# Constant products behind each tile's scores in the four self attentions of a four-layer Perceiver

## The chip, the cores and the metric

One NeuronCore of a Trainium2 chip runs the whole program in one launch. The metric is the device time of that launch in microseconds, and where several runs stand, their median. TensorE is called PE below (its weight loads PEld), VectorE DVE, ScalarE ACT, GpSimd POOL and the queue that issues transfers SP.

## What is computed

The program is a chain of twelve residual blocks on `x` of 32 sequences x 32 tokens x 256 channels, in four layers of cross attention, self attention (or a convolution with pooled keys) and a feed-forward or mixture of experts. The change touches the self attentions only. There are four: in layer 0 (`L0_attn`, causal, scores from three pairs of features), layer 1 (`L1_attn`, relu in place of softmax), layer 3 (`L3_attn`, causal) and, inside the last block, `L3_gqa` (softmax). Cut to the core, each is

```
q, k, v = x @ Wq, x @ Wk, x @ Wv          # 16 heads of 16 channels
a = einsum('bqhd,bkhd->bhqk', q, k) / 4   # 32 x 32 for each sequence and head
a = softmax(where(causal, a, -inf))       # L1_attn: relu(a) / (sum(relu(a)) + 1e-6)
x = x + einsum('bhqk,bkhd->bqhd', a, v) @ Wo
```

## The kernel before

All 1024 tokens lie on chip as 8 tiles (`NT`) of 128 tokens, four sequences to a tile (`BT`). Every block of the network is one or more stages. A stage is a set of five instruction streams, one for each engine, that start together and meet again at its end; within it an engine runs its stream in the order in which it is written, and waits on semaphores where `wait_ge` stands. `prepare` normalises, transposes and projects; `self_attention` follows it.

`self_attention` works through the tiles i = 0 to 7. The order is written out by hand. On PE a tile has five parts:

- `scores(i)` (L1487): small products of 32 rows x 64 columns that sit side by side in the array, 32 of them in float32 (96 in `L0_attn`, with its three feature sets); the causal ones start with 8 products that write the mask (L1479). Their queries are written as block patterns by `spread_queries` on ACT (L1554), DVE (L1616) and POOL (L1599).
- `turn_probs(i)` (L1496): four transposes of the probabilities, which DVE (L1622, L1624) and ACT (L1563, for relu L1560) make from the scores. ACT then copies them out of PSUM (L1570).
- `probs_values(i)` (L1505): 64 products of 32x32 by 17 columns.
- `turn_outputs(i)` (L1512): two transposes of the outputs that DVE normalised (L1634, L1636), copied by ACT.
- `output_product(i)` (L1521): two full products, 128x128 by 256 columns.

The float32 products show in the trace as two matmuls each, the transposes as one. The stream is skewed: with the probabilities of tile i turned, PE does the scores of tile i+1, so that DVE and ACT can make the next probabilities meanwhile; then the outputs of tile i-1 are turned, the values of tile i are multiplied, and the output product of i-1 is made. PSUM bank 6 (`OB`) holds the turned outputs in its first 256 columns; the other 256 are unused. `k.ident` and `k.consts` are constants that stay on chip during the whole program.

All of this is written out for all tiles, without a loop, so that PE's instruction stream is long, and it is itself brought in by transfers from memory (queue q8 of the profile, 16 KB each).

Of the kernel before, what the change touches and what calls it, by code (L numbers as in the profile page):

```python
# [24 lines left out]
B, S, D = 32, 32, 256  # L25
# [267 lines left out]
def spread(ap, n, axis):  # L293

    shape = list(ap.shape)
    return ap.unsqueeze(axis).broadcast_to(shape[:axis] + [n] + shape[axis:])
# [1150 lines left out]
def self_attention(k, w, qt, kt, v, into, causal=False, relu=False, scale=0.25, more=(), after=None):  # L1447

    nc = k.nc
    sets = [(qt, kt), *more]  # L1450
    SB, TB, PB, OB, YB = 0, 4, 5, 6, 7
# [4 lines left out]
    with stage(k, names) as (block, s), \  # L1456
# [13 lines left out]
        @block.tensor  # L1470
        def _(pe):
            def scores(i):
                for done in spread_by:
                    pe.wait_ge(done, i + 1)
                if causal:
                    for r in range(4):
                        rows = slice(r * S, (r + 1) * S)
                        for c in range(DC):
                            nc.tensor.matmul(k.ps[c * 64:(c + 1) * 64, SB + r, 0:P], k.same[rows, :],  # L1479
                                             spread(k.causal[rows, :], BT, 1), start=True, stop=False, skip_group_check=True)  # L1480
                for b_ in range(BT):
                    for m, (_, keys) in enumerate(sets):
                        for r in range(4):
                            rows = slice(r * S, (r + 1) * S)
                            for c in range(DC):
                                own = i * P + b_ * S
                                last = nc.tensor.matmul(k.ps[c * 64:(c + 1) * 64, SB + r, b_ * S:(b_ + 1) * S],  # L1487
                                                        b.qx[rows, i % 2, m, c, b_, :, :], keys[rows, c, own:own + S],
                                                        start=m == 0 and not causal, stop=m == len(sets) - 1,
                                                        skip_group_check=True)  # L1490
                last.then_inc(s.scores_done, 1)

            def turn_probs(i):
                pe.wait_ge(s.probs_ready, i + 1)
                for r in range(4):
                    last = nc.tensor.transpose(k.ps[:, TB, r * P:(r + 1) * P], b.p[:, r, :, :].rearrange("p b l -> p (b l)"),  # L1496
                                               k.ident)
                last.then_inc(s.turned_done, 1)

            def probs_values(i):  # L1500
                pe.wait_ge(s.turned_ready, i + 1)
                for h in range(16):
                    for b_ in range(BT):
                        rows = slice(b_ * S, (b_ + 1) * S)
                        last = nc.tensor.matmul(k.ps[rows, PB, h * 17:(h + 1) * 17], b.pt[rows, h % 8 // 2, h // 8, h % 2, :],  # L1505
                                                v[rows, i, h, :], start=True, stop=True)
                last.then_inc(s.pv_done, 1)

            def turn_outputs(i):
                pe.wait_ge(s.o_ready, i + 1)  # L1510
                for c in range(DC):
                    last = nc.tensor.transpose(k.ps[:, OB, c * P:(c + 1) * P],  # L1512
                                               b.o[:, c * 8:(c + 1) * 8, :].rearrange("p h d -> p (h d)"), k.ident)
                last.then_inc(s.ot_done, 1)

            def output_product(i):
                pe.wait_ge(s.ot_ready, i + 1)
                if i > 0:
                    pe.wait_ge(s.y_added, i)
                for c in range(DC):  # L1520
                    last = nc.tensor.matmul(k.ps[:, YB, 0:D], b.ot[:, c, :], w.wo[:, c, :], start=c == 0, stop=c == DC - 1)  # L1521
                last.then_inc(s.y_done, 1)

            pe.wait_ge(*w.at)
            scores(0)
            pe.wait_ge(s.ones_set, 1)
            for i in range(NT):
                turn_probs(i)
                if i + 1 < NT:
                    scores(i + 1)  # L1530
                if i > 0:
                    turn_outputs(i - 1)
                probs_values(i)
                if i > 0:
                    output_product(i - 1)
            turn_outputs(NT - 1)
            output_product(NT - 1)
            if after == "turned":
                for half in range(2):
                    for t in range(4):  # L1540
                        pe.wait_ge(s.z_ready, half * 4 + t + 1)
                        for c in range(DC):
                            last = nc.tensor.transpose(k.ps[:, 2 * half + c, t * P:(t + 1) * P],
                                                       into[:, half * 4 + t, c * P:(c + 1) * P], k.ident)
                    last.then_inc(s.z_turned, 1)
# [1480 lines left out]
```

## Time and profile before

| | us |
|---|---|
| three runs | 1976.07, 1983.77, 1986.21 |
| median | 1983.77 |
| the profiled execution, its span | 1979.5 |
| `L0_attn`, self attention stage | 300.7 to 400.8 |
| `L1_attn` | 864.5 to 920.1 |
| `L3_attn` | 1683.5 to 1742.4 |
| `L3_gqa` | 1766.8 to 1824.4 |

The times of the stages are from the span's start, in the profiled execution. A "busy" PE counts matmul records; PEclk is the clock that was granted to it, as a share of its full 2.4 GHz, so that 0.50 is 1.2 GHz. "issue" as the reason of a wait means that PE waited for nothing that the profile shows.

### The profile page before, as it was taken

The page shows a single profiled execution, that of the slowest core. Times are in us where ns is not written, and L with a number is a line of the kernel's source. Part 1 is how long each engine was busy: PE and PEld are TensorE (multiplying, and loading weights), DVE is VectorE, ACT ScalarE, POOL GpSimd, SP SyncE. Part 2 cuts the span into 40 slices and gives each one's busy share as a digit, 9 for nine tenths or more (in the row PEclk, how much of TensorE's full clock was granted, in tenths as well). Part 3 has the DMA queues.
Part 4 walks back from the last instruction along what each step waited for, and adds up shares of the span by engine and source line. Part 5 has one row for each costly group of instructions (what it writes and reads, how often), then busy time and mean ns, then how long its engine had stood idle before and what let it go on. Part 6 is the DMA issues. An engine that isn't in the chain of part 4 may idle for free. (4 is left out here: it accounts for less than half of the span.)

```text
span 1979.5 us, 53753 instructions
## 1 busy us (share of the span) xinstructions
PE 1634.6 (83%) x22089; PEld 1401.9 (71%) x22089; DVE 956.7 (48%) x2107; ACT 748.1 (38%) x1700; POOL 447.5 (23%) x627
## 2 busy tenths in 40 slices
PE   6999846769997899887699949997698988778695
PEld 5888645659995777675588848994686966666584
DVE  5565373241115888535512156664666744434313
ACT  3555372123342555432133326663124423333122
POOL 3443102012222434110244322220101200010242
PEclk8999855569998999876699979998898979776697
DMA  4111000049982211001599753331001163000596
GB/s 140 51 52 30 5 1 3 4 177 325 326 316 100 56 51 46 8 6 47 175 311 312 264 182 94 93 89 46 4 19 40 42 199 128 4 2 4 169 306 220
DMA packets 82023, 219.99 MB, mean 111 GB/s; under 512 B 19160, under 2 KB 35032, under 8 KB 74656
## 3 DMA queue, kind: packets, MB, share of 16 engines
q1 hardware_dynamic: 69888, 191.11, 29.6%
q0 software_dynamic: 8160, 22.29, 3.0%
q10 hardware_dynamic: 3776, 3.67, 0.6%
q8 instruction: 158, 2.59, 0.5%
q14 instruction: 41, 0.34, 0.1%
HBM read 201.62 MB, written 15.34 MB: 110 GB/s over the span
## 5 line engine op out<-in xcount | busy, mean ns | idle before, releaser
L2308 PEld LDWEIGHTS ps<-xt,w 128*128 128x128 f32 x1728 | 208.0, 196 | 36.1 <-issue 29.8
L2308 PE MATMUL ps<-xt,w 128*128 128x128 f32 x1728 | 215.9, 282 | 18.7 <-DMA w<-in_L_ffn_w 15.8
L2360 ACT ACTIVATE g<-ps,b 128x128 f32<-128x128 f32 x340 | 124.8, 367 | 247.7 <-PE ps L2308 226.3
L2318 PE MATMUL ps<-w,g 128*128 128x256 f32 x864 | 201.9, 381 | 0.6 <-DMA w<-in_L_ffn_w 0.6
L2318 PEld LDWEIGHTS ps<-w,g 128*128 128x128 f32 x864 | 158.8, 192 | 19.0 <-DMA w<-in_L_ffn_w 1.1
L2396 POOL DMA_INDIRECT x<-rows,token x85 | 83.1, 978 | 261.6 <-DVEq L2496 236.7
L2401 POOL DMA_INDIRECT results<-y,dest x85 | 83.6, 984 | 258.3 <-DVE y L2529 258.3
L2521 DVE COPY xt<-ps 128x256 f32<-128x256 f32 x85 | 36.1, 425 | 202.7 <-PE ps L2298 202.7
L2529 DVE COPY y<-ps 128x256 f32<-128x256 f32 x85 | 36.1, 425 | 162.6 <-PE ps L2318 162.6
L761 PE MATMUL ps<-c,w 128*128 128x258 f32 x512 | 97.2, 302 | 9.9 <-DVE pt L1068 5.9
L761 PEld LDWEIGHTS ps<-c,w 128*128 128x128 f32 x512 | 77.6, 196 | 23.7 <-issue 19.4
L771 PE MATMUL ps<-w,c 128*128 128x256 f32 x512 | 91.2, 291 | 0.0
L897 ACT ACTIVATE p<-sc,nmax 128x257 f32<-128x257 f32 x128 | 58.0, 503 | 80.6 <-DVE nmax L1025 80.6
L407 PE MATMUL ps<-consts_sb,z_sb 128*128 128x128 f32 x176 | 38.8, 411 | 58.4 <-DVE z_sb L591 58.4
L1013 DVE TENSOR_TENSOR val<-ps,store_sb 128x512 f32<-128x512 f32 x64 | 44.2, 690 | 84.7 <-PE ps L771 84.5
L425 PE MATMUL ps<-x,w 128*128 128x512 f32 x336 | 80.7, 399 | 4.5 <-DVE x L603 4.5
L2006 PE MATMUL ps<-x,w 128*128 128x512 f32 x288 | 77.0, 407 | 7.7 <-DVE w L2169 7.7
L570 POOL TENSOR_TENSOR w<-store_sb,w 128x512 fp32r<-128x512 f32 (+1 forms) x20 | 27.0, 1365 | 240.9 <-DVE z_sb L591 205.3
L407 PEld LDWEIGHTS ps<-consts_sb,z_sb 128*128 128x128 f32 x176 | 34.7, 219 | 63.7 <-DVE z_sb L591 63.1
L797 PE MATMUL ps<-consts_sb,p 128*128 128x128 f32 x512 | 74.7, 281 | 5.1 <-ACT key L887 2.2
L2019 PEld LDWEIGHTS ps<-w,g 128*128 128x128 f32 x576 | 74.8, 191 | 5.4 <-issue 1.5
L425 PEld LDWEIGHTS ps<-x,w 128*128 128x128 f32 x336 | 63.7, 192 | 19.6 <-DVE x L603 6.7
(447 smaller groups left out, 3660.7 us busy)
## 6 DMA issues: line engine op xcount, KB each, us to landing
w<-in_L_ffn_w SPq DMA_DIRECT2D x124, 512.0 KB, 5.0
w<-in_L_ffn_w SPq DMA_DIRECT2D x46, 1024.0 KB, 6.0
c<-in_ctx SPq DMA_DIRECT2D x96, 258.0 KB, 2.7
rows<-in_w_L_xattn SPq DMA_DIRECT2D x32, 192.0 KB, 2.6
rows<-in_w_L_xattn SPq DMA_DIRECT2D x8, 768.0 KB
c<-in_w_L_xattn SPq DMA_DIRECT2D x8, 514.0 KB
raw<-in_L_ffn_w SPq DMA_DIRECT2D x16, 256.0 KB, 2.8
tails<-in_w_L_xattn SPq DMA_DIRECT2D x5, 768.0 KB, 7.3
```

Of the source, the lines that this page charges most:

```text
L407: mm = nc.tensor.transpose(k.ps[:, 2 * half + c, t * P:(t + 1) * P], z[:, half * HT + t, c * P:(c + 1) * P], k.ident)
L425: mm = nc.tensor.matmul(bank, r.w[:, p1, c, col:col + P], r.x[:, p2, c, half * 512:(half + 1) * 512], start=i == 0 and c == 0, stop=i == 2 ...
L761: last = nc.tensor.matmul(k.ps[:, KB + c, 0:LP], wp, cp, start=t == 0, stop=t == 4)
L771: last = nc.tensor.matmul(k.ps[:, VB, half * D:(half + 1) * D], cp, wp, start=t == 0, stop=t == 4)
L797: last = nc.tensor.transpose(k.ps[:, TB + pair, at:at + P], b.p[:, par, r4, half * P:(half + 1) * P], k.ident)
L2006: mm = nc.tensor.matmul(k.ps[:, slot(j, h), :], r.w1[:, j // 2, p1, c, h * P:(h + 1) * P], r.x[:, p2, c, (j % 2) * 512:(j % 2 + 1) * 512], ...
L2019: mm = nc.tensor.matmul(k.ps[:, 4 + t, 0:D], r.g[:, p1, slot(j, h), t * P:(t + 1) * P], r.w2[:, j // 2, p2, h, :], start=h == 0 and i == 0 ...
L2308: mm = nc.tensor.matmul(hidden_bank(par, h), b.w1[:, par, c, h * P:(h + 1) * P], b.xt[:, par, c, :], start=c == 0, stop=c == DC - 1)
L2318: mm = nc.tensor.matmul(k.ps[:, YB + par, 0:D], b.g[:, par, h, :], b.w2[:, par, h, :], start=h == 0, stop=h == HC - 1)
L2360: nc.scalar.activation(b.g[:, par, h, :], hidden_bank(par, h), func, bias=b.b1[:, par, h:h + 1]).then_inc(s.g_ready, 1)
L2396: nc.gpsimd.indirect_dma_start(b.x[:, n % 4, :], None, k.rows, bass.IndirectOffsetOnAxis(ap=u.token[:, n:n + 1], axis=0)).then_inc(x_loade ...
L2401: nc.gpsimd.indirect_dma_start(k.results, bass.IndirectOffsetOnAxis(ap=u.dest[:, n:n + 1], axis=0), b.y[:, n % 2, :], None).then_inc(sent[ ...
```

## The change

A helper `keep_awake(n)` issues n float32 products on PE: the identity as the stationary operand, the first 256 columns of the constants as the moving one, into the unused half of PSUM bank 6. Nothing waits for them and nothing reads them. They stand in three places: two at a stage's start, ahead of the wait for the weights; five behind the first tile's scores (two for relu); and two behind the scores of each later tile. That makes 21 products in three of the stages and 18 in `L1_attn`, 81 in all.

```diff
@@ -1521,13 +1521,21 @@
                     last = nc.tensor.matmul(k.ps[:, YB, 0:D], b.ot[:, c, :], w.wo[:, c, :], start=c == 0, stop=c == DC - 1)
                 last.then_inc(s.y_done, 1)
 
+            def keep_awake(n):
+
+                for _ in range(n):
+                    nc.tensor.matmul(k.ps[:, OB, D:2 * D], k.ident, k.consts[:, 0:D], start=True, stop=True)
+
+            keep_awake(2)
             pe.wait_ge(*w.at)
             scores(0)
+            keep_awake(2 if relu else 5)
             pe.wait_ge(s.ones_set, 1)
             for i in range(NT):
                 turn_probs(i)
                 if i + 1 < NT:
                     scores(i + 1)
+                    keep_awake(2)
                 if i > 0:
                     turn_outputs(i - 1)
                 probs_values(i)
```

On PE, at the start of `L0_attn` and behind its first scores (`ps<-consts_sb` of 64x128 is the causal mask, the last row turns the first probabilities):

```order
 L1470 UNCONDITIONAL_BRANCH
+L1527 MATMUL ps<-consts_sb 128x256 x2
 L1479 MATMUL ps<-consts_sb 64x128 x8
 L1487 MATMUL ps<-qk,qx 64x32 x8
...
 L1487 MATMUL ps<-sn,qx 64x32 x8
 L1487 MATMUL ps<-cs,qx 64x32 x8
+L1527 MATMUL ps<-consts_sb 128x256 x5
 L1496 MATMUL ps<-consts_sb,p 128x128 x4
```

Two products now stand ahead of the first scores and five between the first scores and the transposes that wait for the first probabilities.

On PE, one tile inside `L1_attn` before:

```order
L1496 MATMUL ps<-consts_sb,p 128x128 x4
L1487 MATMUL ps<-kt,qx 64x32 x32
L1512 MATMUL ps<-consts_sb,o 128x128 x2
L1505 MATMUL ps<-v,pt 32x17 x64
L1521 MATMUL ps<-store_sb,ot 128x256 x2
```

and the same tile now:

```order
L1496 MATMUL ps<-consts_sb,p 128x128 x4
L1487 MATMUL ps<-kt,qx 64x32 x32
L1527 MATMUL ps<-consts_sb 128x256 x2
L1512 MATMUL ps<-consts_sb,o 128x128 x2
L1505 MATMUL ps<-v,pt 32x17 x64
L1521 MATMUL ps<-store_sb,ot 128x256 x2
```

The two products come between the scores of the next tile and the turned outputs of the last one; nothing else on PE changes its place, and the other engines' streams are the same.

## Rows read from the trace of the kernel before

**Rows 1.** The page: span, and the clock granted to PE in 40 slices.

```profile
span 1979.5 us, 53753 instructions
...
PEclk8999855569998999876699979998898979776697
```

**Rows 2.** Stretches, the four stages: length, busy time (count) of PE, PEld, DVE, ACT, POOL, PEclk, DMA.

```profile
300.70:400.80 100.10, 72.59 (x2768) 60.50 (x2768) 28.08 (x70) 21.85 (x43) 15.06 (x17) 0.55 0.01 4
...
864.50:920.10 55.60, 49.85 (x1619) 40.07 (x1617) 19.30 (x53) 18.31 (x41) 5.67 (x2) 0.57 0.02 4
...
1683.50:1742.40 58.90, 46.89 (x1744) 38.16 (x1744) 23.11 (x54) 21.85 (x43) 0.32 (x1) 0.70 0.02 4
...
1766.80:1824.40 57.60, 46.48 (x1616) 37.68 (x1616) 21.88 (x53) 21.57 (x42) 4.69 (x2) 0.61 0.02 4
```

**Rows 3.** Stretches of one tile, L1496 to L1496, and sums of seven: L0_attn.

```profile
332.50:344.46 11.96, 8.69 (x348) 0.64 0.02 4
344.46:356.12 11.66, 9.18 (x347) 0.50 0.01 3
...
sum 81.28, PE 60.98; mean PE 8.71
```

**Rows 4.** The same of L1_attn, all engines.

```profile
887.86:894.28 6.42, 6.42 (x204) 5.19 (x203) 2.28 (x7) 2.25 (x5) 0.00 (x0) 0.50 0.01 3
...
sum 45.32, PE 43.43 PEld 35.31 DVE 12.10 ACT 14.66 POOL 3.75; mean PE 6.20 PEld 5.04 DVE 1.73 ACT 2.09 POOL 0.54
```

**Rows 5.** The same of L3_attn.

```profile
1693.93:1700.89 6.96, 6.96 (x225) 5.74 (x219) 2.75 (x6) 2.38 (x5) 0.00 (x0) 0.50 0.02 5
...
1720.32:1725.55 5.23, 4.33 (x219) 3.68 (x218) 3.01 (x7) 2.38 (x5) 0.00 (x0) 1.00 0.03 6
...
sum 45.71, PE 37.83 PEld 31.36 DVE 18.64 ACT 15.52 POOL 0.00; mean PE 5.40 PEld 4.48 DVE 2.66 ACT 2.22 POOL 0.00
```

**Rows 6.** The same of L3_gqa.

```profile
sum 44.18, PE 40.51 PEld 32.96 DVE 17.94 ACT 15.52 POOL 0.00; mean PE 5.79 PEld 4.71 DVE 2.56 ACT 2.22 POOL 0.00
```

**Rows 7.** Timeline of PE, L1_attn: start, length, line, shape, count [idle before].

```profile
885.99 2.07 PE L1521 MATMUL ps<-store_sb,ot 128*128 128x256 f32 x4
887.86 1.06 PE L1496 MATMUL ps<-consts_sb,p 128*128 128x128 f32 x4
```

**Rows 8.** Timeline of PE, L3_attn (clock 1.00 until past 1728.60).

```profile
1723.74 0.91 PE L1505 MATMUL ps<-v,pt 32*32 32x17 f32 x87 [0.90 <-issue]
1724.58 1.13 PE L1521 MATMUL ps<-store_sb,ot 128*128 128x256 f32 x4
1725.55 0.60 PE L1496 MATMUL ps<-consts_sb,p 128*128 128x128 f32 x4
1726.08 0.47 PE L1479 MATMUL ps<-consts_sb 32*64 32x128 f32 x16
1726.35 0.29 PE L1487 MATMUL ps<-kt,qx 32*64 32x32 f32 x16
1727.58 0.72 PE L1487 MATMUL ps<-kt,qx 32*64 32x32 f32 x48 [0.94 <-issue]
1728.23 0.44 PE L1512 MATMUL ps<-consts_sb,o 128*128 128x128 f32 x2
1728.60 0.84 PE L1505 MATMUL ps<-v,pt 32*32 32x17 f32 x78
1731.05 0.88 PE L1505 MATMUL ps<-v,pt 32*32 32x17 f32 x50 [1.61 <-issue]
```

**Rows 9.** Waits of PE in L0_attn: us in total, times, longest.

```profile
PE ps L1487 <- issue: 11.5, 8, 2.1
PE ps L1479 <- POOL qx L1599: 8.7, 1, 8.7
PE ps L1505 <- issue: 8.0, 7, 1.3
PE ps L1496 <- ACT p L1563: 2.3, 1, 2.3
```

**Rows 10.** Waits of PE in L3_gqa.

```profile
PE ps L1496 <- ACT p L1563: 5.4, 1, 5.4
```

## The prediction

> **What bounds the kernel now.** I first read the span and the row of the granted clock [rows 1]: PE is at full clock for most of the program, and slices 7 and 8, in which `L0_attn` lies, are among the lowest, with 5 tenths. Next I cut out the four stages that the change touches [rows 2]. They take 100.1, 55.6, 58.9 and 57.6 us, 272.2 us of 1979.5, and PE's clock in them is 0.55, 0.57, 0.70 and 0.61. PE is the busiest engine in each; DVE, ACT and POOL are busy for less than half. So PE's stream sets their length, and the rest of the program isn't touched.
>
> Within PE there are two limits, and the reader has to see both. The first is the clock. In `L1_attn` a tile takes 6.42 us with PE busy for 6.42 of them, at 0.50 [rows 4]: nothing waits, the engine is just slow. The same groups are quicker at full clock: from the start of the output product to the start of the next transposes it is 1.87 us at 1.2 GHz [rows 7] and 0.97 us at 2.4 GHz [rows 8].
>
> The second limit shows as soon as the clock is full. At 1.00, a tile of `L3_attn` has 4.33 us of work but takes 5.23 [rows 5], and the timeline has waits for "issue" of 0.90, 0.94 and 1.61 us [rows 8]. They aren't scattered: from the end of one to the start of the next there are 87+4+4+16+16 = 127 matmuls, then 48+2+78 = 128, and the ends are 3.84 and 3.47 us apart. Such a regular count speaks for the stream being brought in by pieces of 128 matmuls with their weight loads, each 3.65 us behind the last at best. In `L0_attn` these waits are 11.5 + 8.0 us of the 100 [rows 9], and a tile at clock 0.64 isn't shorter (11.96) than one at 0.50 (11.66) [rows 3]. There a faster array only waits longer.
>
> **The added products at one tile.** Two float32 products of 128x128 by 256 columns are what the output product is. I take them at the same 1.87 us for a pair at 1.2 GHz and 0.97 at 2.4 GHz [rows 7, 8]. PE is the engine that everything waits for, so by themselves they are paid in full where PE has no waits, as in `L1_attn`, and hidden where a wait for instructions stands behind them, since the next piece comes in meanwhile. They add 4 matmuls to a piece's count, which is small. DVE isn't held: the semaphore of the scores is raised by the last score, ahead of the added products.
>
> **What they do to the clock.** The change takes nothing away, so a gain can only come from here. In the trace, the clock rises after stretches in which full-array work lies close together, and falls after stretches of scores and values, small products that leave most of the array idle even where PE is busy the whole time: in `L1_attn` the seven tiles had PE busy for 43.43 of 45.32 us [rows 4] and nearly all at 0.50. A tile now has one such stretch, the output product and the next transposes, 8 matmuls. With the pair behind the scores it has a second, half a tile away. I expect that this lifts the clock early in a stage and then mostly holds it, as it already held for one whole tile of `L3_attn` (1.00) with half the work [rows 5]. I take 9 tiles of 10 at full clock in `L1_attn`, `L3_attn` and `L3_gqa`; the bounds are all and none.
>
> The Trainium skill, "TensorE: Matmul & The Clock Gate" ("Why this matters for your kernels"), speaks against this change: it ties the full clock to keeping TensorE busy without gaps. By that rule a PE that is busy already, as in `L1_attn`, gains nothing from more work. The tile at 6.42 us busy of 6.42 and at 0.50 doesn't agree with the rule as a matter of busy time alone; where it held, the sum would be the rival of the cold clock below.
>
> **The sum.** At full clock, a tile is the longer of its work and its pieces. Work: 4.33 us in `L3_attn` [rows 5] + 0.97 = 5.3; less in the others, which have no mask. Pieces: `L1_attn` and `L3_gqa` have 202 matmuls in a tile and now 206, so 206/128 x 3.65 = 5.9 us; `L3_attn` has 222, so 6.3 us. The pieces win. At half clock, a tile is 6.42 + 1.87 = 8.3 us, and 6.96 + 1.87 = 8.8 us in `L3_attn` [rows 4, 5].
>
> - `L1_attn`: 45.32/7 = 6.47 us a tile now [rows 4]. Full: 7 x (5.9 - 6.47) = -4.0; half: 7 x 1.83 = +12.8. With 9 to 1: -2.3 us.
> - `L3_gqa`: 44.18/7 = 6.31 [rows 6]. Full: -2.9; half: +13.9. With 9 to 1: -1.2 us.
> - `L3_attn`: 45.71/7 = 6.53 [rows 5], it was at 0.70 already. Full: -1.6; half: +16. With 9 to 1: +0.2 us.
> - `L0_attn`: 81.28/7 = 11.61 [rows 3]. Waits for pieces in front of the values are 8.0/7 = 1.14 us a tile [rows 9]; they stand right behind the new pair. At half clock 1.87 - 1.14 = 0.73 shows, at full clock 0.97 is hidden. This stage has few output products for its length, and I leave it mostly at half clock: +0.5 a tile, +3.5 us. Bounds: +13 (nothing hidden, 7 x 1.87) and -3 (the clock rises and some of it isn't eaten by the pieces).
> - The starts. The first pair is hidden: PE waits 8.7 us for POOL's queries in `L0_attn` [rows 9]. The five behind the first scores take 2.5 x 1.87 = 4.7 us at half clock. In `L3_gqa` they lie in a wait of 5.4 us [rows 10], hidden. In `L0_attn` the wait for the first probabilities is 2.3 us [rows 9] and the clock is low: +2.4. In `L3_attn` the clock is full and they take 2.4 us, which about fills the same wait; `L1_attn`, with two, pays some 0.2.
>
> Sum: -2.3 - 1.2 + 0.2 + 3.5 + 2.4 + 0.2 = +2.8 us on the execution of 1979.5, which lies 4.3 below the median of the runs. On the median of 1983.8 it gives 1986.6; I say 1986.
>
> **The rivals.** *The clock stays low* (slower). The pair doesn't lift it, or only as often as now. Then each of the three short stages pays its half-clock figure, 12.8 + 13.9 + 16, of which `L3_attn` and `L3_gqa` hide a part in their present waits for pieces (some 7 in all), and `L0_attn` 7 x 0.73 + 2.4 = 7.5: about +43, 2027 us. For it: the tile in `L1_attn` that is busy throughout at 0.50. Against: the clock does rise in these stages, after the output products, and the pair is of that shape. Half of it (the clock up for 6 tiles of 10) would give some +20, 2004; the point from which it shows as slower is about 7 tiles of 10 at full clock.
>
> *The pieces aren't a floor* (faster). If the waits for instructions shrink because the added products give the transfers time, tiles come near their work at full clock: 5.3 us in `L3_attn` and some 4.9 in the two others, which is 7 x (1.2 + 1.6 + 1.4) = -29, and with `L0_attn` at -3 some -30: 1954. Half of it is 1969. For it: 4.33 us of work in the tile at 1.00. Against: the two ends 3.84 and 3.47 us apart, which a product in between doesn't shorten.
>
> *The change does not reach the time*: the products are nearly all hidden and the clock as now; that is within 5 us of the median too and is counted with "same".
>
> **How the numbers follow.** A measurement of this kernel can tell about 0.5%, 10 us, from no change. My forecast and its near neighbours, 1974 to 1994: 0.58. The faster rival in whole or in part: 0.20. The clock too low, in whole or in part: 0.22. Range: from 1966 (half of the faster one) to 2006 (half of the slower one), which leaves out about 0.1 at each side.
>
> **What would show it.** In the profile after: the added line with 162 matmuls; the clock in the four stages (I expect 0.9 or more in the three short ones, and 0.6 to 0.75 in `L0_attn`); tiles of 5.8 to 6.3 us with waits for "issue" left, some 128 matmuls apart. Tiles over 8 us with PE busy throughout at 0.50 would show the slower rival, tiles under 5.5 us the faster one. The forecast is wrong in its first step if another stage than these four moves by more than the few us that separate the runs.

## The result and the profile after

The changed kernel takes 1970.08 us (median of 20 runs, 1961.32 to 1981.43), the one before 1978.79 us (20 runs, 1969.25 to 1986.73). The ratio is 0.9962 with a 95% interval of 0.9947 to 0.9977: 7.5 us faster, by 4.6 to 10.5. The forecast was 1986 and a small loss. The time lies inside the range, but the sign was wrong, and by more than the interval.

The page after, span and granted clock, against [rows 1]:

```profile
span 1966.9 us, 54077 instructions
...
PEclk9999956779998999888799969998898989988697
```

The four stages, cut as in [rows 2] (length, busy time and count of PE, PEld, DVE, ACT, POOL, then PEclk and DMA):

```profile
300.10:394.10 94.00, 73.94 (x2810) 61.31 (x2810) 28.04 (x71) 20.98 (x42) 15.06 (x17) 0.72 0.02 4
850.40:907.50 57.10, 48.44 (x1655) 38.72 (x1654) 19.24 (x53) 18.33 (x41) 5.69 (x2) 0.85 0.02 4
1671.20:1726.70 55.50, 46.78 (x1786) 38.34 (x1786) 23.82 (x55) 20.97 (x42) 0.32 (x1) 0.97 0.02 4
1750.90:1810.10 59.20, 49.98 (x1658) 40.39 (x1658) 22.56 (x55) 20.97 (x42) 4.71 (x2) 0.83 0.02 4
```

The clock rose in all four, from 0.55, 0.57, 0.70 and 0.61 to 0.72, 0.85, 0.97 and 0.83. But the stage that I had given a loss of 6 us, `L0_attn`, is 6 us shorter, and `L1_attn`, with a much higher clock, is no shorter at all. (The last two stretches begin with the first added products, 1 us ahead of where they began before. From ACT's first query pattern to the last output product the four stages take 93.4, 55.7, 54.4 and 58.2 us, against 99.4, 54.2, 58.8 and 57.5.)

The added line in the list of groups, and what PE waited for in `L0_attn`, against [rows 9] (us in total, times, longest):

```profile
L1527 PE MATMUL ps<-consts_sb 128*128 128x256 f32 x162 | 55.4, 479 | 8.3 <-PEq L223 8.3
```

```profile
PE ps L1487 <- issue: 13.2, 7, 2.3
PE ps L1527 <- PEq L223: 5.1, 1, 5.1
PE ps L1479 <- issue: 3.2, 6, 0.7
PE ps L1505 <- issue: 1.6, 2, 0.9
```

55.4 us of matmuls were added to a program that became shorter. The waits for instructions in front of and inside the values (L1505) fell from 8.0 to 1.6 us: the pair lies where they were. Those at the scores didn't fall (11.5 and 1.5 us before, for L1487 and for L1479; 13.2 and 3.2 now).

Two traces don't settle a few us. Stages that the change does not touch differ as well between them: the products of `L1_xattn`'s cross attention, from the first to the last on PE, took 207.2 us in the trace before, 6.9 us less in the one after, and 1.4 to 6.0 us less in those of the five experiments of the whole program below, none of which touches it. So the experiments measure the whole program many times, or the same stage several times in one trace.

### The profile page after: what moved, and what is told of

Same layout as the page of the kernel before. It is cut to its first block and busy times, and to the rows that moved or that the text cites. A ratio compares the mean times of both kernels' runs of the same rounds, so it can differ in the third digit from the quotient of the medians.

```text
span 1966.9 us, 54077 instructions
## 1 busy us (share of the span) xinstructions
PE 1633.8 (83%) x22251; PEld 1397.4 (71%) x22251; DVE 956.8 (49%) x2107; ACT 746.9 (38%) x1700; POOL 447.0 (23%) x627
## 5 line engine op out<-in xcount | busy, mean ns | idle before, releaser
L897 ACT ACTIVATE p<-sc,nmax 128x257 f32<-128x257 f32 x128 | 58.0, 503 | 80.5 <-DVE nmax L1025 80.5
L407 PE MATMUL ps<-consts_sb,z_sb 128*128 128x128 f32 x176 | 39.3, 415 | 58.8 <-DVE z_sb L591 58.8
```

What stands on the lines that cost most here:

```text
L407: mm = nc.tensor.transpose(k.ps[:, 2 * half + c, t * P:(t + 1) * P], z[:, half * HT + t, c * P:(c + 1) * P], k.ident)
```

## The experiments

Ratios are to the kernel before, run on the same chip; the experiments were spread over two chips. "A stage" is from ACT's first query pattern to the last output product.

### In which stage is the gain?

Two kernels share the added products out. The first keeps them in `L0_attn` only, the second everywhere else.

```diff
-                for _ in range(n):
+                for _ in range(n if len(sets) > 1 else 0):      # e1_first_only
+                for _ in range(n if len(sets) == 1 else 0):     # e2_not_first
```

> The added products stand in L0_attn alone (21 of the 81). Theory 1 (the step of my sum that failed is L0_attn: its clock rises from 0.55 to about 0.7, and the rise is not eaten by the waits for instructions): L0_attn, 99.5 us from its first query pattern to its last output product, comes down to 93 to 95, and the program is at a ratio of 0.996 to 0.998. Theory 2 (L0_attn gains nothing, as predicted, and the gain is made in the short stages or between the stages): L0_attn at 99 or more, ratio 1.000 to 1.003.

> The added products stand in L1_attn, L3_attn and L3_gqa and not in L0_attn. Theory 1: the three stages together are within 3 us of before, the ratio is 0.998 to 1.001. Theory 2: the ratio is near 0.996, as with the whole change.

`L0_attn` alone: 1975.02 us, ratio 0.9973 (0.9952 to 0.9993). The other three alone: 1976.08 us, ratio 0.9985 (0.9961 to 1.0009). The two add up to what the whole change gives (0.27% + 0.15% and 0.38%). So there is a gain in the one stage to which I had given the largest loss, and the first theory stands in its direction. That it is the larger part of the whole isn't shown: the two intervals overlap, and the second one holds no change as well. The size in this one trace, 97.9 us against 99.4, was smaller than expected; the four-fold runs below give 2.9 us.

### The starts

The pair behind the scores of tiles 1 to 7 is dropped, and the products at the stage's start and behind its first scores are kept.

```diff
                     scores(i + 1)
-                    keep_awake(2)
```

> Only the products at the start of each stage and behind its first scores (25 of the 81), none in the later tiles. If the clock is held by the pair of each tile: after the first tiles the clock is as before, the stages gain at most 1 to 2 us each, ratio 0.998 to 1.001. Rival, that lifting the clock once at the start is what counts: ratio near 0.996.

1982.75 us, ratio 1.0008 (0.9986 to 1.0031). Lifting the clock once gives nothing that can be measured. The gain needs the pairs; whether they would do without the products at the starts no run shows.

### The array's work or only the time?

The same number of products of the same length, but in one corner of the array:

```diff
-                    nc.tensor.matmul(k.ps[:, OB, D:2 * D], k.ident, k.consts[:, 0:D], start=True, stop=True)
+                    nc.tensor.matmul(k.ps[0:32, OB, D:2 * D], k.ident[0:32, 0:32], k.consts[0:32, 0:D], start=True, stop=True)
```

> The whole change, but each added product uses 32 rows and 32 columns of the array, by the same 256 columns of data: the same number of matmuls and the same length of each (an estimate from the wide ones: 1.9 us a pair at 1.2 GHz), with a sixteenth of the array at work. Theory of the clock: it stays as low as before or lower (0.5 to 0.6 in the four stages), every tile is 1 to 2 us longer, and the program is 25 to 45 us slower (ratio 1.013 to 1.023). Rival, that the products help by giving the instruction transfers time, whatever they compute: ratio 0.996, like the change.

1989.27 us, ratio 1.0058 (1.0037 to 1.0080): slower by 11 us, and about 1% slower than the wide products. The sign is the clock theory's; the size is less than half of what I expected of it, and it isn't the rival's 0.996 either. The clock that I had expected, 0.5 to 0.6 in all four stages, was so in `L0_attn` alone: the trace has 0.58, 0.78, 0.66 and 0.75. How much of that is the one trace shows in the next set.

### Four samples of each stage

To see a stage by itself, each of the four self attention stages is run four times in a row, in the kernel before, in the change, and in two variants. The output is then another one, the stages are not.

```diff
-                    self_attention(k, w, b.qk[:, 0], ...)
+                    for _ in range(4):
+                        self_attention(k, w, b.qk[:, 0], ...)   # and the same for the three others
```

> The kernel before with each of the four self attention stages run four times in a row, so that one trace holds four samples of each stage with the clock in different positions (the output is then not the reference's). It is the baseline for the three next. Stages as before within 3 us: L0_attn 99, L1_attn 50 to 54, L3_attn 55 to 59, L3_gqa 57 to 60, and the program some 3 x 265 = 800 us longer.

> The change, with each self attention stage run four times in a row (output not the reference's). If the gain lies in the stages themselves, it shows four times: 4 x 5 to 9 us = 20 to 36 us less than the same kernel before, half of it in the four passes of L0_attn (3 to 5 us each). If most of it came from the stages behind them or from chance, 0 to 10 us less.

> The same with narrow products (32 rows and 32 columns of the array), each self attention stage four times (output not the reference's). Clock theory: the clock in the stages is below the wide ones' by 0.1 or more and each stage is 4 to 8 us longer than with wide ones. Rival (the products only give the instruction transfers time): the same as the wide ones within 1 us a stage.

> The change with the pair of each tile moved from behind the scores to behind the output product, each self attention stage four times (output not the reference's). If the place in front of the values is what hides the pair (it lies in the wait for instructions there), L0_attn is 3 to 6 us longer than with the pair behind the scores, and has its waits of 1.1 us in front of or inside the values back. If only the full-array work counts, it is the same within 1 us.

The last one has the pair moved:

```diff
                 if i + 1 < NT:
                     scores(i + 1)
-                    keep_awake(2)
...
                 if i > 0:
                     output_product(i - 1)
+                if i + 1 < NT:
+                    keep_awake(2)
```

The medians are 2839.37 us (before), 2816.86 (change), 2909.29 (narrow) and 2872.35 (behind the output product). All four ran on one chip. The change is 22.5 us faster, which is 5.6 for each pass through the four stages; the narrow products are 70 us slower than none, and the pair in the other place 33 us slower. Means of the four passes of a stage, in us, with the clock:

| | before | change | narrow | behind output |
|---|---|---|---|---|
| `L0_attn` | 97.3, 0.58 | 94.4, 0.71 | 103.0, 0.58 | 99.0, 0.71 |
| `L1_attn` | 54.3, 0.67 | 55.4, 0.84 | 58.1, 0.70 | 58.6, 0.79 |
| `L3_attn` | 59.1, 0.67 | 55.1, 0.96 | 64.8, 0.68 | 60.5, 0.87 |
| `L3_gqa` | 56.0, 0.68 | 57.1, 0.87 | 61.5, 0.69 | 59.4, 0.84 |
| sum | 266.7 | 262.0 | 287.4 | 277.5 |

The passes of one stage in one trace lie 2 to 6 us apart (`L0_attn` in the change: 91.9, 94.1, 97.2 and 94.3), so a mean of four is good to 1 us or so, as an estimate. The losses of 1.1 us in `L1_attn` and `L3_gqa` are no larger than that.

The stretch of the four passes of `L0_attn`, with the columns of [rows 2]; before, change, narrow, behind the output product:

```profile
301.20:694.40 393.20, 278.88 (x11072) 233.81 (x11072) 113.82 (x285) 87.00 (x171) 59.81 (x68) 0.58 0.02 4
```

```profile
301.20:682.90 381.70, 302.04 (x11240) 249.41 (x11240) 113.69 (x285) 84.61 (x171) 60.06 (x68) 0.71 0.02 4
```

```profile
300.00:716.40 416.40, 346.31 (x11240) 253.98 (x11240) 113.68 (x285) 84.95 (x172) 60.05 (x68) 0.59 0.01 4
```

```profile
298.80:699.00 400.20, 306.64 (x11240) 254.30 (x11240) 113.86 (x286) 87.14 (x171) 59.80 (x68) 0.71 0.02 4
```

The four passes of `L3_attn` with the narrow products:

```profile
2203.80:2467.20 263.40, 246.12 (x7144) 174.26 (x7144) 95.44 (x221) 84.64 (x171) 1.29 (x4) 0.68 0.01 4
```

And the waits for instructions in `L0_attn`, in the order of its four rows:

```profile
PE ps L1487 <- issue: 49.6, 32, 2.2
PE ps L1505 <- issue: 30.0, 29, 2.3
PE ps L1479 <- issue: 6.3, 24, 0.4
```

```profile
PE ps L1487 <- issue: 48.7, 27, 2.4
PE ps L1479 <- issue: 11.1, 25, 0.7
PE ps L1505 <- issue: 6.0, 8, 1.4
```

```profile
PE ps L1487 <- issue: 48.1, 30, 2.3
PE ps L1479 <- issue: 6.6, 24, 0.5
PE ps L1505 <- issue: 2.5, 3, 1.4
```

```profile
PE ps L1505 <- issue: 41.9, 28, 2.6
PE ps L1487 <- issue: 37.8, 31, 2.3
```

Read across, these rows take the change apart into two mechanisms:

- *Place.* Behind the scores, wide or narrow, the pair takes the wait at the values from 30.0 us to 6.0 or 2.5. Behind the output product, at the same clock of 0.71, the wait is 41.9, and `L0_attn` is 4.6 us a pass longer. Over all four stages the place is worth 15.5 us a pass (277.5 against 262.0), but in the other three the clock is lower as well (0.79, 0.87 and 0.84 against 0.84, 0.96 and 0.87), so only `L0_attn` shows the place by itself.
- *The array's work.* Narrow and wide products stand in the same place and take the same time: in `L0_attn`, from the start of a pair to the next transposes, 1.84 us narrow and 1.87 wide where the clock is at 0.50, 0.98 and 0.97 where it is at 1.00. With the narrow ones the clock stays at 0.58 to 0.70, the values of before, and the four stages take 25.4 us more a pass. PE was busy for 346.31 of 416.40 us in `L0_attn` with the narrow products and only for 302.04 of 381.70 with the wide ones, and the clock was the lower one of the two; in `L3_attn` it was 246.12 of 263.40 us, at 0.68, and 188.26 of 224.70 us with the wide ones, at 0.96. Time occupied isn't what the clock follows. A narrow product has fewer rows, fewer columns and a smaller weight load (123 ns against 190 in the median); which of the three counts isn't shown.

With narrow products each stage was to be 4 to 8 us longer than with wide ones; it was 2.7 to 9.7. In the single kernel they cost 11 us and not 20.7 (287.4 - 266.7), beyond its interval of 7 to 16. The four stages aren't the reason: in the trace of that kernel they take 287.2 us together, as here. What is outside them takes 1701.7 us there and 1709.5 in the trace of the kernel before; in the traces of the change and of the other variants that part, which none of them touches, is between 1705.2 and 1717.0. Why it was short with the narrow products stays open.

### How many products?

One product and four instead of the pair, again in four passes:

```diff
-                    keep_awake(2)
+                    keep_awake(1)      # x4_one;  x4_four: keep_awake(4)
```

> One added product behind each tile's scores, each self attention stage four times (output not the reference's). If the clock needs the pair, it falls back half way (L3_attn 0.8, L0_attn 0.65) and L3_attn is at 56 to 58 us, L0_attn at 94.5 to 96. If one is enough, the clock stays at 0.96 and 0.71, and all four stages are as with the pair or up to 2 us shorter.

> Four added products behind each tile's scores in place of two, each self attention stage four times (output not the reference's). If 128 matmuls of the stream can't come in faster than in some 3.65 us and this bounds L3_attn at full clock (6.3 us a tile, with work of 5.3), the second pair's 0.97 us a tile is mostly hidden: L3_attn 55 to 57.5 us against 55.1 with one pair. If the tile is bound by its work, 7 x 0.97 is added: 61 to 62 us. L0_attn has nearly no wait left in front of its values, so there the second pair shows: 98 to 101 us against 94.4.

One: 2849.70 us; four: 2837.12 us; none was 2839.37 and two 2816.86. But these two kernels ran twice each, on another chip, where the single kernel before takes 1980.22 us and not 1975.49. As ratios to that, none, one, two and four are 1.4368, 1.4387, 1.4273 and 1.4324, each to within 0.006 to 0.008, which doesn't tell one or four products from none. By stage (none, one, two, four): `L0_attn` 97.3, 98.9, 94.4, 97.6; `L1_attn` 54.3, 56.3, 55.4, 55.4; `L3_attn` 59.1, 59.3, 55.1, 54.9; `L3_gqa` 56.0, 56.6, 57.1, 59.0.

The four passes of `L3_attn`, with no product, one, two and four:

```profile
2172.80:2413.50 240.70, 190.63 (x6976) 156.42 (x6976) 95.39 (x222) 87.10 (x171) 1.28 (x4) 0.67 0.02 4
```

```profile
2179.90:2421.50 241.60, 204.99 (x7088) 164.73 (x7088) 95.37 (x221) 86.90 (x172) 1.30 (x4) 0.80 0.02 4
```

```profile
2158.70:2383.40 224.70, 188.26 (x7144) 153.32 (x7144) 95.44 (x221) 84.48 (x171) 1.29 (x4) 0.96 0.02 4
```

```profile
2175.10:2398.80 223.70, 204.95 (x7256) 170.97 (x7256) 95.36 (x222) 84.62 (x171) 1.29 (x4) 0.99 0.02 4
```

The last two rows are the test of the floor in my forecast. The second pair adds 16.7 us of busy PE and the stretch gets 1 us shorter: at full clock a tile of `L3_attn` was not bound by its work. Taken alone, the tiles went from 6.28 to 6.40 us, which is what four more matmuls cost at 128 in 3.65 us (0.11); the stage's start and end made up for it. Its waits for instructions with two and with four products show where the pair went:

```profile
PE ps L1505 <- issue: 21.9, 24, 1.5
PE ps L1487 <- issue: 5.7, 11, 0.9
```

```profile
PE ps L1487 <- issue: 7.1, 13, 1.2
PE ps L1505 <- issue: 3.4, 6, 1.5
```

21.9 became 3.4. The waits themselves bear out the pieces: with two products there are 36 "issue" waits in these four passes, and from each to the next within its pass there are one or two times 128 matmuls (to within one). Where it is 128, 24 times, they are 3.47 to 4.02 us apart, in the median 3.75. One product isn't half of two in `L0_attn`: it leaves the clock at 0.60 and only costs its time. I had expected 0.65 and 94.5 to 96 us there, and 56 to 58 in `L3_attn`, for 98.9 and 59.3; with four products the two stages came out just below what I expected.

### Only where it pays

In four passes the products gained in the two causal stages, and seemed to cost in the two others. The five behind the first scores of `L0_attn` put its first transposes 1.9 us later (12.0 us behind the start, against 10.1). So the last kernel has them in the causal stages only, with two there instead of five.

```diff
-                for _ in range(n):
+                for _ in range(n if causal else 0):
...
-            keep_awake(2 if relu else 5)
+            keep_awake(2 if len(sets) > 1 else 5)
```

> The added products only in the two causal stages, L0_attn and L3_attn, and in L0_attn two behind the first scores in place of five. In the four-fold runs these two stages gained 2.9 and 4.0 us with the products and the other two lost 1.1 each, and the five cost L0_attn 1.9 us at its start. Expected: 7 to 9 us less than before, ratio 0.9955 to 0.9965, at or below the whole change. If the four-fold stages don't stand for the single ones: 0.998 or more.

1973.98 us, ratio 0.9955 (0.9934 to 0.9976). With 39 products in place of 81 it is as fast as the change; the intervals overlap, so which of the two is better isn't settled. In its trace `L0_attn`'s first transposes are 9.6 us behind the start, so the 1.9 us are back, but the stage took 97.0 us, at a clock of 0.62.

The single traces warn against the four-fold losses. In the kernel with the products everywhere but in `L0_attn`, `L1_attn` took 47.6 us; the same stage with the same products took 55.7 us in the trace of the change, at 0.85:

```profile
862.40:910.00 47.60, 41.01 (x1652) 33.62 (x1652) 18.51 (x52) 18.30 (x41) 5.67 (x2) 1.00 0.02 4
```

Over all traces, single and four-fold, that have either all of a stage's products or none of them, the mean with against without is 94.8 against 97.9 us for `L0_attn`, 55.3 against 58.3 for `L3_attn`, 54.2 against 54.3 for `L1_attn` and 57.3 against 56.5 for `L3_gqa`. So the gain in the two causal stages stands, and a loss in the two others isn't shown.

## Why the prediction was wrong

**What bounds the kernel** held. PE's stream sets the four stages, and its limits are the clock and the coming in of instructions.

**`L0_attn` is the step that failed.** I wrote that there "a faster array only waits longer", kept the stage "mostly at half clock" and charged +3.5 us for the tiles and +2.4 for the start. My own sign for the profile, a clock of 0.6 to 0.75 in place of 0.55, was met (0.72), but the sum had nothing for that rise. Over four passes, seven tiles take 76.4 us against 80.5, so -0.58 us a tile and not +0.5. The start was sized nearly right (+1.9). Of the tile, three terms can be read from the four-fold traces: the pair costs 1.62 us from its start to the next group's, the mean of the 28 pairs of four passes; the wait at the values falls by (30.0 - 6.0)/28 = 0.86 (I had 1.14 at most); the wait at the scores grows by (59.8 - 55.9)/28 = 0.14. That leaves -0.58 - 1.62 + 0.86 - 0.14 = -1.48 us a tile, which I put down to the clock (0.58 to 0.71) and for which my sum had nothing. Narrow products in the same place, with the clock at 0.58, make the same seven tiles 83.3 us and not 76.4. The evidence that I used against it was one pair of tiles, 11.96 us at 0.64 and 11.66 at 0.50 [rows 3]. Two tiles out of a stage in which a tile varies between 9.3 and 12.4 us couldn't carry that: the waits eat some of a faster array, 0.14 us a tile, not all of it.

**`L3_attn`** was right in its mechanism. A tile takes 43.99/7 = 6.28 us at a clock of 0.96, where I had 6.3, and that this is the pace at which instructions come in is shown by the second pair, which costs next to nothing, and by the count of 128 between the waits. The term was still mis-sized, +0.2 for -4.0. The tile before is 46.93/7 = 6.70 us over four passes, not 6.53 as in the one trace [rows 5]; I had charged one tile in ten at half clock and 8.8 us, which none of the 28 was; and I had left out the stage's end, where the last output products come 1.4 us sooner at full clock.

**`L1_attn` and `L3_gqa`** didn't gain: -2.3 and -1.2 forecast, +1.1 each measured in four passes, -0.1 and +0.8 over all traces. "9 tiles of 10" at full clock was too many (0.84 and 0.87), and the 5.9 us were not reached (6.33 and 6.27 a tile). Where `L1_attn` did stay at 1.00, in the 47.6 us above, its seven tiles took 38.95 us, 5.56 each. So 5.9 is not a floor of a short stage either; why it can fall below isn't shown. The gain against before was overrated too, since one trace had 6.47 and 6.31, four passes 6.29 and 6.04. Of `L1_attn`'s loss, 1.5 us is in its start, which in the program itself isn't longer (2.81 against 2.93 us), so there the stage is about even. That fits with the ratio of the kernel that leaves out `L0_attn`.

**The sum's two slips.** The half of the faster rival is 1969 in one place and 1966 in another, and with `L0_attn` at -3 its 29 us make 32 and not 30; neither changes the forecast.

**The rivals.** That the clock stays low was wrong for the wide products and is what the narrow ones do. That the pieces aren't a floor was wrong in `L3_attn`. The rule of the Trainium skill that I weighed ("TensorE: Matmul & The Clock Gate", "Why this matters for your kernels") ties the full clock to a busy TensorE. In these stages the runs don't agree with it as a matter of time occupied: 83% busy at a clock of 0.59 with narrow products, 79% at 0.71 with wide ones.

The chances had a gain of over 0.5% at 0.20 and no change within it at 0.58. The measured 0.38% is in the second. Read as times it isn't: 1970.08 lies below the 1974 to 1994 to which I gave 0.58, since the kernel before, too, was faster over 20 runs (1978.79) than over the three I had (1983.77). That the time fell inside the whole range is partly luck. What was wrong is the sum, whose terms of the three short stages came from one trace each, and that of the long one from two tiles.

## What to carry to other kernels

Where a stage of small products keeps TensorE at half clock, full-array products that nobody reads can pay, if they stand where the engine would wait anyway; behind the scores here, in front of the values, and not behind the output product. Count the waits for "issue" first: their pace, 128 matmuls in 3.5 to 4.0 us here, says both how much can be hidden and how little a faster array can bring. And take the time of a stage whose clock goes up and down from several passes, since one trace was off by more than the whole effect.

## What the runs showed of the hardware

- Two products of the same length differ in what they do to the clock: 32 rows x 32 columns of the array left it at 0.58 in `L0_attn`, 128 x 128 brought 0.71, and in `L3_attn` 0.68 against 0.96.
- More products gave a higher clock in every stage. With none, one, two and four it was 0.67, 0.80, 0.96 and 0.99 in `L3_attn`, and 0.58, 0.60, 0.71 and 0.77 in `L0_attn`, where the first one did next to nothing.
- At full clock the second pair of products in a tile of `L3_attn`, 16.7 us of busy time in four passes, cost next to nothing (223.7 us against 224.7, the tiles alone 0.12 us each), and its waits for instructions fell from 27.6 to 10.5 us.
- One stage with the same instructions took from 47.6 to 55.7 us (`L1_attn` with the pairs, single traces), at a clock of 1.00 and 0.85.
